# Attention and mixture of experts on one core: attended values kept by feature, placed by DMA, normalised four heads at a time

## The reference, cut to what matters

```python
xn = layernorm(x)                          # x is (2, 1024, 512) f32
out = x + attention(xn) + ffn(xn)

# attention: 16 heads of 32 features, causal, per batch b and head h
Q, K, V = (split_heads(xn @ W.T) for W in (Wq, Wk, Wv))
P = softmax(where(causal, Q @ K.T / sqrt(32), -1e30))
O = P @ V                                  # divided by the row sums of exp
attention = merge_heads(O) @ Wo.T

# ffn: 8 experts of 352, top 2 of grouped scores, weights * 2.5,
# and a shared expert of 704:  silu(x @ g.T) * (x @ u.T) @ d.T
```

## Time and profile before

| what | us |
|---|---|
| median of 3 runs | 1119.6 (1117.81 to 1122.33) |
| the profiled execution | 1127.01 |
| its span, first to last instruction | 1125.0 |
| PE busy in the span | 1046.2 (93%) |
| VectorE busy | 784.6 (70%) |
| ScalarE busy | 637.9 (57%) |
| GpSimd busy | 506.4 (45%) |
| mean granted clock of TensorE | 0.969 of 2.4 GHz |

### The profile page before, as it was taken

How to read it: one execution, slowest core, us unless ns; L and a number is a source line. 1 busy time by engine, 2 the same in 40 slices (tenths; PEclk the granted TensorE clock), 3 DMA queues, 4 the chain that set the end, 5 groups by cost and what they waited for, 6 DMA issues and landing times. The chain is left out here.

```text
span 1125.0 us, 18890 instructions
## 1 busy us (share of the span) xinstructions
PE 1046.2 (93%) x5379; PEld 817.6 (73%) x5380; DVE 784.6 (70%) x1675; ACT 637.9 (57%) x1278; POOL 506.4 (45%) x568
## 2 busy tenths in 40 slices
PE   6999979888899998999999999998989999999994
PEld 4767867666677776777778777776867777778872
DVE  6732324565688887788888888865568888888872
ACT  3323211265588786787787887872155555565550
POOL 0013903388756564556566565651013443333321
PEclk9999989988899999999999999998989999999997
DMA  6989996255543553644445426118789444443432
GB/s 213 322 335 361 136 293 231 94 67 102 132 133 77 150 148 75 163 118 136 115 113 151 126 64 191 45 39 266 243 283 278 90 76 75 75 72 68 71 54 35
DMA packets 106201, 163.61 MB, mean 145 GB/s; under 512 B 53984, under 2 KB 64480, under 8 KB 102656
## 3 DMA queue, kind: packets, MB, share of 16 engines
q1 hardware_dynamic: 95776, 141.82, 44.1%
q0 software_dynamic: 9760, 20.49, 10.0%
q10 hardware_dynamic: 576, 0.26, 0.1%
HBM read 101.25 MB, written 61.28 MB: 144 GB/s over the span
## 5 line engine op out<-in xcount | busy, mean ns | idle before, releaser
L1198 POOL TENSOR_TENSOR prob_lo<-prob,prob_hi 128x512 fp32r<-128x512 f32 (+2 forms) x320 | 308.3, 977 | 203.3 <-ACT prob_hi L1243 147.0
L1236 ACT ACTIVATE prob<-ps_s 128x512 f32<-128x512 f32 (+3 forms) x384 | 188.0, 490 | 127.1 <-PE ps_s L1463 77.1
L1243 ACT ACTIVATE prob_hi<-prob 128x512 fp32r<-128x512 f32 (+3 forms) x384 | 198.6, 517 | 12.4 <-ACT row_stage L1217 12.4
L1862 DVE TENSOR_TENSOR rw_lo<-gu_sb,rw_hi 128x704 fp32r<-128x704 f32 x156 | 138.8, 893 | 52.7 <-ACT rw_hi L1806 47.7
L1306 DVE CUSTOM_DVE_ANT_0 ps_m<-ps_m,causal 128x384 f32<-128x384 f32 (+3 forms) x256 | 126.7, 495 | 69.2 <-PE ps_m L1432 66.9
L1806 ACT ACTIVATE rw_hi<-gu_sb 128x704 fp32r x156 | 123.5, 794 | 62.8 <-PE ps_ru L1895 43.6
L1458 PE MATMUL ps_s<-qs,ks 97*128 97x512 f32 (+3 forms) x384 | 140.4, 366 | 9.4 <-ACT prob L1236 9.2
L1779 POOL DMA_INDIRECT out<-work,slot_table x39 | 63.5, 1627 | 181.1 <-DVE work L1847 148.2
L1481 PE MATMUL ps_o<-prob_hi,vs 128*66 128x512 f32 (+3 forms) x384 | 133.1, 347 | 10.4 <-issue 9.6
L1432 PE MATMUL ps_m<-ks,qs 96*128 96x512 f32 (+3 forms) x384 | 139.1, 362 | 0.6 <-DVE maxima L1306 0.2
L1483 PE MATMUL ps_o<-prob_lo,vs 128*66 128x512 f32 (+3 forms) x384 | 132.0, 344 | 0.0
(11 more groups left out here) (201 smaller groups left out, 2353.0 us busy)
## 6 DMA issues: line engine op xcount, KB each, us to landing
xt<-xt_blocks SPq DMA_DIRECT2D x7, 2048.0 KB, 9.1
v_rows<-work SPq DMA_DIRECT2D x16, 512.0 KB, 3.0
xt_blocks<-xt SPq DMA_DIRECT2D x4, 2048.0 KB, 11.3
qk_hi<-work SPq DMA_DIRECT2D x8, 1024.0 KB, 4.7
qk_lo<-work SPq DMA_DIRECT2D x8, 1024.0 KB, 7.5
qs<-qk_hi SPq DMA_DIRECT2D x64, 128.0 KB, 2.9
ks<-qk_hi SPq DMA_DIRECT2D x64, 128.0 KB, 3.2
vs<-v_rows SPq DMA_DIRECT2D x32, 256.0 KB, 4.7
```

The source lines that it names most:

```text
L1198: nc.gpsimd.tensor_tensor(prob_lo[:, s % NPL, 0:w], prob[:, s % NP, 0:w], prob_hi[:, s % NPH, 0:w].bitcast(F32), ALU.subtract).then_inc(lo ...
L1236: nc.scalar.activation(prob[:, s % NP, 0:w], ps_s[s % NS][:, 0:w], ACT.Exp, scale=SCALE).then_inc(exp_done, 1)
L1243: nc.scalar.activation(prob_hi[:, s % NPH, 0:w], prob[:, s % NP, 0:w], ACT.Copy).then_inc(hi_ready, 1)
L1862: nc.vector.tensor_tensor(w_lo[:, k, :], chunk(e, k), w_hi[:, k, :].bitcast(F32), ALU.subtract).then_inc(w_lo_ready, 1)
```

## The change

Outputs are no longer turned. `o_copy` stays features by queries, and SP places it by DMA: the 32 high rows of each head go into `attended`, now 128 features (four heads side by side) by queries, the 32 low rows into `o_low`, and the row of sums to DRAM and from there, spread over 32 partitions, into `o_den`. The order of the heads becomes four heads of one batch, then the same four of the other. When the fourth head is there, VectorE adds, takes the reciprocal of the spread sums and multiplies, each on 128x512. The output projection takes `attended` as it is.

Besides, SP's program goes by steps, not by heads, the values have two slots instead of four, and the planner no longer counts 270 for a turn.

```diff
+def head_of(g):
+    return QUAD * (g // (QUAD * B)) + g % QUAD, g // QUAD % B
...
-    COPY, TURN, NORM = VALUE + 1, VALUE + 2, VALUE + 3
+    COPY, PLACE, SPREAD, NORM = VALUE + 1, VALUE + 2, VALUE + 4, VALUE + 6
...
-        if 0 <= s - TURN < STEPS and (s - TURN) % NB in ENDS:
-            cost += 270
...
-    XT_AT = [None] + [head_after(step_of(unit - 1, UP_END[-1] - 1)) for unit in range(1, UNITS)]
-    ACC_AT = [1] + [head_after(step_of(unit - 1, PER_UNIT - 1) + 1) for unit in range(1, UNITS)]
-    RAW_AT = [2] + [head_after(min(SPLIT_AT, key=lambda s: SPLIT_AT[s] != [k - 1]) + 1)
-                    for k in range(1, NF)]
+    XT_AT = {step_of(unit - 1, UP_END[-1] - 1) + 1: unit for unit in range(1, UNITS)}
+    STORE_AT = {step_of(unit, PER_UNIT - 1) + 2: unit for unit in range(UNITS)}
+    BASE_AT = {0: 0, **{s + 4: unit + 1 for s, unit in STORE_AT.items() if unit + 1 < UNITS}}
+    RAW_AT = {NB: 0, **{s + 2: ks[0] + 1 for s, ks in SPLIT_AT.items() if ks[0] + 1 < NF}}
...
+                def place_output(s):
...
+                    sp.wait_ge(o_copied, 2 * g + half + 1)
...
+                    for into, rows in ((attended[at, tiles, h // QUAD, :], slice(0, DK)),
+                                       (o_low[at, half], slice(DK, 2 * DK))):
+                        sp.dma_start(into, o_copy[rows, half, :].rearrange("p (a q) -> p a q", a=4)
+                                     ).then_inc(o_placed[half], 16)
+                    o = 2 * g + half
+                    sp.dma_start(den_dram[o:o + 1, :], o_copy[2 * DK:2 * DK + 1, half, :]
+                                 ).then_inc(den_saved, 16)
...
+                def spread_sums(s):
...
+                    sp.wait_ge(den_saved, 16 * (o + 1))
+                    sp.dma_start(o_den[n * DK:(n + 1) * DK, half].rearrange("p a q -> p (a q)"),
+                                 den_dram[o:o + 1, :].broadcast_to([DK, TBW])
+                                 ).then_inc(o_placed[half], 16)
...
+                for s in range(ALL):
+                    if s % NB == 0 and HS <= s // NB + 1 < HEADS:
+                        next_head(s // NB + 1)
...
+                    if s % NB == NB // 2 and V_SLOTS <= s // NB - 1 < HEADS:
+                        load_values(s // NB - 1)
+                    if 0 <= s - PLACE < STEPS:
+                        place_output(s - PLACE)
+                    if 0 <= s - SPREAD < STEPS:
+                        spread_sums(s - SPREAD)
...
-                    wait(act, o_turned, o - 1)
+                    wait(act, o_placed[half], 48 * g)
...
+                def finished(s):
+                    return s % NB in ENDS and s // NB % QUAD == QUAD - 1
+
+                def sum_outputs(s):
...
+                    dve.wait_ge(o_placed[half], 48 * (g + 1))
+                    nc.vector.tensor_tensor(of, of, o_low[:, half], ALU.add).then_inc(normalizing, 1)
+                    nc.vector.reciprocal(o_den[:, half], o_den[:, half]).then_inc(normalizing, 1)
+
                 def normalize(s):
...
+                    dve.wait_ge(normalizing, 2 * (2 * (g // QUAD) + half + 1))
+                    nc.vector.tensor_tensor(of, of, o_den[:, half], ALU.mult).then_inc(o_ready, 1)
...
-                    for lag, stage in ((NORM, normalize), (0, maximum), (LO, lo),
-                                       (NORM + 1, weigh_o)):
+                    for lag, stage in ((0, maximum), (LO, lo), (NORM, sum_outputs),
+                                       (NORM + 1, normalize)):
...
-                    for lag, stage in ((TURN, turn_o), (0, maximum), (ROW, turn_row)):
+                    for lag, stage in ((0, maximum), (ROW, turn_row)):
...
-                pipeline(dve, NT, U, [(0, copy), (1, lo), (1, split_wo), (2, add)])
+                pipeline(dve, NT, U, [(0, lo), (0, split_wo), (1, add)])
...
-                pipeline(pe, NT, U, [(0, turn), (1, multiply)])
+                pipeline(pe, NT, U, [(0, multiply)])
```

More of the change, by code:

```diff
@@ L97, in moe_attention_kernel @@
     slots_dram = nc.dram_tensor("slots", [NSLOT, 2], F32, kind="Internal").ap()
+    den_dram = nc.dram_tensor("sums", [2 * B * H, TBW], F32, kind="Internal").ap()
     xt_dram = nc.dram_tensor("xt_blocks", [NTB, P, 2, KC, TBW], F32, kind="Internal").ap()
@@ L912, in attend_phase @@
         started = sbuf("started", [P, NST, E])
-        slot = sbuf("slot", [P, NT, E])
-        pick = sbuf("pick", [P, NT, E])
+        slot, pick = [started[:, n * NT:(n + 1) * NT, :] for n in range(2)]
         before = sbuf("before", [P, NT, E])
@@ L943, in attend_phase @@
         o_copied = sem("o_copied")
-        o_turned = sem("o_turned")
-        o_read = sem("o_read")
+        o_placed = [sem(f"o_placed{n}") for n in range(2)]
+        den_saved = sem("den_saved")
         normalizing = sem("normalizing")
@@ L1033, in _ @@
                                      ).then_inc(table_loaded, 16)
[L1034 to L1043, removed]
-                        if g == RAW_AT[k]:
-                            load_gate_up(k)
-                        if g == DOWN_RAW_AT[k]:
-                            load_shared_down(k)
-                store_acc(UNITS - 1)
                 sp.wait_ge(acc_stored, 64 * UNITS)
@@ L1423, in _ @@
             def _(pe):
-                turned = {"rows": 0, "outputs": 0}
                 def maximum(s):
@@ L1441, in turn_row @@
                     wait(pe, row_ready, g)
-                    wait(pe, o_read, turned["outputs"])
                     nc.tensor.transpose(ps_row[0:QT, :], maxima[:, c, 0:QT],
                                         ident[:, :]).then_inc(row_turned, 1)
-                    turned["rows"] += 1
                 def score(s):
@@ L1484, in value @@
                                      stop=n in ENDS).then_inc(pv_done, 1)
-                def turn_o(s):
-                    if s % NB not in ENDS:
-                        return
-                    o = 2 * (s // NB) + BLOCKS[s % NB][0]
-                    pe.wait_ge(o_copied, o + 1)
-                    wait(pe, o_read, o)
-                    wait(pe, row_ready, turned["rows"])
-                    for q in range(4):
-                        last = nc.tensor.transpose(ps_ot[:, q, 0:VW], o_copy[:, o % 2, q * P:(q + 1) * P],
-                                                   ident[0:VW, 0:VW])
-                    last.then_inc(o_turned, 1)
-                    turned["outputs"] += 1
                 def gate_or_up(unit, m):
@@ L1581, in out_phase @@
         wo_lo = sbuf("wo_lo", [P, KC, D], F32R)
-        a_tile = sbuf("a_tile", [P, R, D])
         a_hi = sbuf("a_hi", [P, R, KC, P], F32R)
         a_lo = sbuf("a_lo", [P, R, KC, P], F32R)
-        ps_t = [psum(f"ps_at{n}", [P, KC, P]) for n in range(R)]
         ps_y = [psum(f"ps_ay{n}", [P, D]) for n in range(R)]
@@ L1674, in split_wo @@
                                                     ALU.subtract).then_inc(wo_lo_ready, 1)
-                pipeline(dve, NT, U, [(0, copy), (1, lo), (1, split_wo), (2, add)])
+                pipeline(dve, NT, U, [(0, lo), (0, split_wo), (1, add)])
             @block.tensor
             def _(pe):
-                def turn(i, c):
-                    t = U * i + c
-                    wait(pe, tile_ready, t + 1)
-                    wait(pe, lo_ready, t - R + 1)
-                    for k in range(KC):
-                        last = nc.tensor.transpose(ps_t[c % R][:, k, :], a_tile[:, c % R, k * P:(k + 1) * P],
-                                                   ident[:, :])
-                    last.then_inc(turned, 1)
                 def multiply(i, c):
```

127 lines of the change are left out of this document (63 added, 64 removed).

## The result

| | median of the runs, us | range |
|---|---|---|
| before | 1120.4 | 1117.8 to 1122.3 (4 runs) |
| changed | 1179.6 | 1176.1 to 1184.4 (4 runs) |

The ratio is 1.0533, with a 95% interval of 1.0489 to 1.0577: slower, by 59 us. The forecast was 1170, with a range of 1125 to 1202. The profiled execution took 1180.4, its span is 1178.6 and its mean granted clock 0.943 (before: 0.969).

A forecast was written before the change was run, and what follows sets the result against it. TensorE, busy 93% of the span, was taken as the bound. The terms 68.6 + 3 + 11.3 - 17.4 - 8.4 - 6.8 gave +50.3 us, so 1170 us as a median, 4.5% slower; range 1125 to 1202.

The forecast's parts named there:

- lumps: VectorE's addition, reciprocal and product on 128x512, once per four heads and half: 14 cost TensorE 4.9 us each, 68.6 us.
- tail: End of attention after the last copy: two DMA legs and three VectorE operations make it 13.0 us, adding 11.3 us.
- late sums: Sums going to DRAM and back reach VectorE late in half 0: 0.5 us on 7 groups, 3 us.
- SP by steps: Raw-weight loads issued 10 and 11 steps ahead end ScalarE's waits of 1.23 and 1.80 us in two heads: 8.4 us saved.
- turns: Turn groups removed from attention on TensorE: 58 at 0.30 us each, 17.4 us saved.
- projection: Turns removed from the output projection: 0.45 us a tile for 15 tiles, 6.8 us saved, less if `y_tile` transfers lag.
- The reciprocal: VectorE's new reciprocal of 128x512: 4.4 us taken, from estimates between 0.69 and 4.7 us.
- rival A: The reciprocal streams in about 0.69 us and TensorE does not stop: 1095 us, chance 0.14.
- The stop: TensorE, two `maximum` products ahead, stands 3.2 us behind VectorE's addition and reciprocal, then loses 1.7 us to a lower clock.
- Rival B: The reciprocal takes 3.2 us, TensorE stands 2.0 us and loses 2.9 us each of 14 times: 1141 us, chance 0.15.
- Rival C: SP's queue delays the spread sums, so VectorE and TensorE wait 3 us more each time: 42 us more, 1212, chance 0.09.
- Rival D: The turns in attention were free and removing them brings nothing: +17 us, 1187; no separate chance given.

The follow-up runs named there:

- later: The changed kernel with VectorE's addition, and all behind it, three steps later: 1158.1 us, ratio to before 1.0332.
- norecip: The changed kernel without its sixteen reciprocals, outputs multiplied by the sums instead: 1113.2 us, ratio to before 0.9945.
- folded_late: The kernel `folded` with the transfer of the inverses, their spreading and the product two, four and five steps later: 1109.0 us, ratio to before 0.9888.
- before_sp_steps: The kernel before with only SP's program by steps and two value slots, its turns kept: 1113.0 us, ratio to before 0.9931.
- folded: The changed kernel with four heads' sums reloaded as 128x16 for one short reciprocal, inverses spread from DRAM, last group direct: 1128.8 us, ratio to before 1.0050.
- The pieces: The changed kernel with each reciprocal cut into eight, one a step: 1158.2 us; the same three steps later: 1152.8; cut into two: 1166.1.

## Why the prediction was right, point by point

**The sum.** It gave +50.3 us, and +59 were measured (58.1 against the median of before in the first group of runs, which the table uses). The runs split it so:

| part | forecast | measured |
|---|---|---|
| the reciprocals by themselves (14 lumps of 4.9, and 4.4 in the tail) | +73.0 | +44.9 (later against norecip), or +52 (fourteen by `folded_late`, and 3.3 in the tail) |
| late sums ahead of them | +3 | at most +21.5 (changed against later, which holds the place of the lumps too) |
| SP by steps | -8.4 | -8.5 (before_sp_steps against before) |
| turns -17.4, projection -6.8, tail without its reciprocal +6.9 | -17.3 | about 0 (norecip against before_sp_steps), its own stops behind late sums included; -7 if the lumps are taken at +52 |

The sign, the place and the mechanism are right. That the total is right to 9 us is in part luck: by the first figures two sizes in it were off by 28 and 18 us in opposite directions, and the last row by 17.

**The reciprocal** was mis-sized. I took 4.4 us from eight times an addition's time per element; it took 3.34. That is (3341 - 254) / 496 = 6.2 ns an element beyond the 16 of the earlier trace rows, close to the lower slope there, from 1 to 16 elements (6.0). The eight times was a comparison of two instructions of one length, 254 ns, in which the fixed parts are hidden. The Trainium skill's "VectorE: DVE Perf Modes" gives a repeat count of 8 in its walkthrough of the pipeline, which as 8 cycles an element would be 4.3 us at the page's clock (the prediction's estimate). The page does not say that an element takes 8 cycles, and this trace disagrees with that reading: it measures six such cycles an element. The other reading, a stream at 0.69 us, is ruled out, and rival A with it.

**The stop.** The mechanism holds as written: addition and reciprocal behind one reading, two `maximum` free, then a stop, in pairs, every four heads, from 310 us on. In the kernel `later`, where little else adds to it, the stop is 2.35 us on average. Rival B had 2.0 for this reciprocal, and its 2.9 us a lump is close to the lower of the two measured sizes (3.0 and 3.5). For the clock I had 1.7 us a stop, from two windows behind another stop; 0.6 to 1.2 are left in the runs. The window of the earlier trace rows that I charged in full also holds a part of the stop itself, and a low clock costs nothing while TensorE stands. Whether this is the difference was not tested.

**Why the time was still the forecast's and not B's 1141**: the late sums and the place of the lumps, and gains that did not come (below). I had put 3 us on late sums. The two legs can take less than I assumed: in the tail the sums of the last head were there 4.75 us after the copy's end (808.79 to 813.54), not 7.2. The Trainium skill's "DMA: Bandwidth & Descriptors", in its anatomy of one DMA, gives about 2.0 us as a DMA's fixed cost, measured on the path of DMAs that GpSimd issues; two of them and 0.8 of issue would be 4.8 (my estimate). This trace agrees in the sum, for DMAs that SP issues, and roughly in the parts: 1.3 us to the issue of the store, 1.4 from there to the issue of the spread, and 2.0 from that to its use.

```profile
808.20 0.59 ACT L1290 ACTIVATE o_copy<-ps_o 66x512 f32<-66x512 f32 x1 [2.85 <-PE ps_o L1509]
...
813.54 0.69 DVE L1378 TENSOR_TENSOR work<-work,o_low 128x512 f32<-128x512 f32 x1 [1.57 <-DMA o_den<-sums]
814.15 3.35 DVE L1379 RECIPROCAL o_den<-o_den 128x512 f32<-128x512 f32 x1
817.53 0.69 DVE L1388 TENSOR_TENSOR work<-work,o_den 128x512 f32<-128x512 f32 x1
```

But in half 0 the spread stands on SP's queue behind the six loads of a head, as the prediction said, and can come late there. The spread that VectorE waited for at 671.64 was issued at 666.91, so it took 4.7 us from its issue to its use, against 2.0 in the tail:

```profile
666.45 0.42 SPq L198 DMA_DIRECT2D ks<-qk_hi  x1
666.91 0.42 SPq L1023 DMA_DIRECT2D o_den<-sums  x1
```

So most of its delay came after its issue; that the six loads ahead of it caused this is inferred, not tested. Such a wait holds up the same readings as the lump, and the two add to one stop (5.98 us). Moving the addition, and the lump with it, three steps gave back 21.5 us. This is the step that was sized most wrongly: a term of 3 us stood for one of up to 21.5. Rival C had 42 us for such a wait in every lump; it came in five of sixteen.

**The turns.** What their removal gives is not settled. From the first to the last value product attention takes 522.3 us in `before_sp_steps`, which still has the turns, 524.2 without them in `norecip`, and 515.8 in `folded_late` (one trace each). So in `norecip` nothing is left of the 17.4 us of the forecast. A part went into the waits for the sums: even with no reciprocal VectorE waits 15.0 us for them, and one such wait of 4.18 us makes a TensorE stop of 2.81. In `folded_late`, where most of that is cured, 6.5 us are gained. It would be about 12 (my estimate) without its stop of 2.96 us and the two of 1.75 described below, where `before_sp_steps` has one of 0.87. Rival D, that the turns were free, does not fit these 6.5 us, but the changed kernel came out on balance as if they had been.

**The raw weights.** ScalarE's waits are gone from the changed kernel, and in `before_sp_steps` the stretch from 380 to 460 us shows a full clock, so that step is right. In the changed kernel a different stop took their place. Two splits now stand right ahead of the copy of an output. TensorE's next product into that buffer starts when the copy ends, 1.75 us late, and the same happens once more. The view names no releaser ("issue"), so the cause is read from the times:

```profile
424.58 0.62 ACT L1315 ACTIVATE sg_hi<-gu_raw 128x512 fp32r<-128x512 f32 x1
425.10 0.61 ACT L1315 ACTIVATE su_hi<-gu_raw 128x512 fp32r<-128x512 f32 x1
425.62 0.58 ACT L1290 ACTIVATE o_copy<-ps_o 66x512 f32<-66x512 f32 x1
```

```profile
426.29 0.41 PE L1507 MATMUL ps_o<-prob_hi,vs 128*66 128x512 f32 x1 [1.75 <-issue]
```

**Tail and projection.** From the copy's end to the end of attention it is 9.4 us, before 1.7: +7.7 where I had +11.3 (shorter legs, shorter reciprocal). From there to the first matmul of the routed stage it is 57.6 us (818.2 to 875.84), before 60.2 (760.27 to 820.51): -2.6 where I had -6.8. The first product starts 4.4 us after the end of attention in both kernels, and a matmul in the stream takes 0.227 us, 2.72 a tile, as foreseen. Of the 4.2 us that are missing 2.4 are one stop after the eleventh tile, where VectorE had waited 4.87 us for a load of `y_tile`; the granted clock from 852 to 862 us was 0.88.

```profile
857.45 0.69 DVE L1671 TENSOR_TENSOR y_tile<-ps_ay,y_tile 128x512 f32<-128x512 f32 x1 [4.87 <-DMA y_tile<-out]
858.06 0.68 DVE L1663 TENSOR_TENSOR a_lo<-work,a_hi 128x512 fp32r<-128x512 f32 x1
```

```profile
858.80 0.50 PE L1694 MATMUL ps_ay<-wo_hi,a_hi 128*128 128x512 f32 x1 [2.38 <-DVE a_lo L1663]
```

This is the case that the forecast gave "between 0 and 6.8". Tail and projection together are +5.1, forecast +4.5, again by two errors that cancel.

## What to carry to other kernels

Price a new instruction on an in-order engine by how long it keeps a reader that the bound engine needs waiting, not by its busy time: here the same 70 us of work cost 9 us spread out and 60 us in rows. Before making an operation "wider and rarer", ask what the wide one does per element; if it does not stream, reshape its input (512 sums a head as 128x16) rather than cut it up. And when a step is moved, list who waits for its result on the other queues, and what it comes to stand beside on its own. The pieces moved a product onto a wait of SP and into a row with an addition, and their first times were about that.

## What the runs showed of the hardware that was not expected

- VectorE's reciprocal: 164 ns for one element a partition, 254 for 16 (243 in `folded`), 537 for 64, 1736 for 256, 3341 for 512. That is 6.2 ns for each element beyond a fixed part of about 0.15 us; a product of 512 takes 681 ns.
- A small store to DRAM and the load back, with both issues on one queue, took 4.75 us from the end of the copy to the use, less than two of the smallest loads that the trace of before had (3.2 us each). The load back alone took 2.0 us from its issue to its use there, and 4.7 behind the six loads of a head.
- The granted clock of the 20 us windows that hold one of TensorE's stops in `later` was 0.90 or 0.91 in thirteen of fourteen, and 1.00 in the other; it was 0.84 in a window of the changed kernel that holds two. The time lost beyond the stops was 0.6 to 1.2 us each.
